# A Flamingo block with a mixture of experts on one core: the last batch's two head groups are worked side by side

## The reference, cut to what matters

```python
def _L1_xattn_ref(q, k, v):          # q: tokens x features, k = v = context
    qh = q.reshape(b * h, d // h, m)     # h = 8 heads of 32 tokens each
    qk = jnp.einsum('bdm,bdn->bmn', qh, kh) * scale
    sm = jax.nn.softmax(qk, axis=-1)     # 512 x 512 for each head
    ret = jnp.einsum('bmn,bcn->bcm', sm, vh)
    return ret.reshape(b, c, m)

def _L1_ffn_ref(x, w_gate, w_shared_up, w_shared_down, w_up, w_down):
    su = x_flat @ w_shared_up            # the shared expert
    y_s, g_s = jnp.split(su, 2, axis=-1)
    shared = jax.nn.silu(g_s) * y_s @ w_shared_down
    scores = jax.nn.sigmoid(x_flat @ w_gate)
    _, topk_idx = jax.lax.top_k(scores, TOPK)
    ...
    pos = jnp.take_along_axis(jnp.cumsum(oh, axis=0), flat_e[:, None], axis=1)[:, 0] - 1
    x_disp = jnp.zeros((E, CAP, C), x.dtype).at[flat_e, pos].set(x_flat[token_ids], mode='drop')
```

## Time and profile before

| what | value |
|---|---|
| three runs | 1053.34, 1055.82, 1057.88 us (median 1055.82) |
| the profiled execution | 1054.74 us, of which the trace's span is 1053.0 us |
| PE busy | 993.8 us (94%) |
| DVE, ACT, POOL busy | 603.7, 335.0, 465.5 us |
| last batch's own stretch | about 643 to 723 us of the span |

### The profile page before, as it was taken

How to read it: one execution, slowest core, us unless ns; L and a number is a source line. 1 busy time by engine, 2 the same in 40 slices (tenths; PEclk the granted TensorE clock), 3 DMA queues, 4 the chain that set the end, 5 groups by cost and what they waited for, 6 DMA issues and landing times.

```text
span 1053.0 us, 15353 instructions
## 1 busy us (share of the span) xinstructions
PE 993.8 (94%) x5629; PEld 606.8 (58%) x5630; DVE 603.7 (57%) x1249; ACT 335.0 (32%) x491; POOL 465.5 (44%) x457
## 2 busy tenths in 40 slices
PE   7999899999999999999999998895999999999887
PEld 6986445554554564564464462344777777776432
DVE  3334454675765765855846756743655556553566
ACT  3411023323224133233223332442434444443221
POOL 1000023724756657567577553462355555556000
PEclk9999899999999999999999999997999999999999
DMA  8893268598682581590530327556899999965998
GB/s 316 292 390 115 83 221 333 206 346 329 222 303 100 190 309 45 193 350 1 188 116 32 103 80 305 204 210 253 300 370 383 376 370 372 372 250 214 376 417 324
DMA packets 93622, 262.23 MB, mean 249 GB/s; under 512 B 10454, under 2 KB 10582, under 8 KB 92784
## 3 DMA queue, kind: packets, MB, share of 16 engines
q1 hardware_dynamic: 43760, 146.18, 38.0%
q10 hardware_dynamic: 31872, 63.97, 16.2%
q0 software_dynamic: 17920, 51.15, 12.4%
HBM read 129.91 MB, written 139.72 MB: 256 GB/s over the span
## 4 chain that ended last, share of the span: by engine, by line
PE 71%; DVE 7%; POOL 7%; DMA 7%; issue 4%; ACT 3%; SPq 0%; POOLq 0%; ACTq 0%; DVEq 0%
PE banks L1266 17%; PE banks L1861 11%; PE banks L1276 10%; PE banks L1850 6%; DMA e_eo<-y_d 6%; PE banks L1870 6%; POOL t_psum L766 5%; PE banks L1364 5%; PE banks L1426 5%; PE banks L1444 2%; DVE t_nmx L1057 2%; ACT t_probs L857 2%; PE banks L396 1%; PE banks L402 1%; PE banks L407 1%
## 5 line engine op out<-in xcount | busy, mean ns | idle before, releaser
L1684 POOL DMA_INDIRECT y_d<-e_eo,e_ids x128 | 124.5, 972 | 126.7 <-DVE e_eo L1781 94.0
L1057 DVE TENSOR_REDUCE t_nmx<-banks 128x4 f32<-128x2048 f32 x56 | 128.1, 2288 | 61.2 <-PE banks L1364 61.2
L766 POOL TENSOR_TENSOR t_psum<-t_psum,t_probs 128x512 f32<-128x512 f32 x104 | 128.5, 1267 | 63.4 <-ACT t_probs L857 62.6
L857 ACT ACTIVATE t_probs<-banks 128x2048 f32<-128x2048 f32 x56 | 105.2, 1878 | 141.0 <-PE banks L1429 117.1
L778 POOL DMA_INDIRECT xs_d<-r_norm,r_xaddr x96 | 96.4, 1004 | 46.5 <-issue 24.9
L736 POOL TENSOR_TENSOR f_rstd<-f_veps,mhalf 128x2 f32<-128x2 f32 x24 | 16.8, 699 | 149.0 <-DVE f_veps L955 149.0
L1426 PE MATMUL banks<-b_qry,b_key 32*128 32x512 f32 x512 | 73.0, 639 | 7.8 <-ACT t_probs L857 5.7
L1850 PEld LDWEIGHTS banks<-ident,e_xg 128*128 128x128 f32 x512 | 57.4, 144 | 32.6 <-issue 32.5
L1850 PE MATMUL banks<-ident,e_xg 128*128 128x128 f32 x512 | 64.4, 281 | 10.9 <-DMA e_xg<-xs_d 10.9
L766 POOL TENSOR_TENSOR t_psum<-t_probs,t_probs 128x512 f32<-128x512 f32 x52 | 66.5, 1315 | 12.1 <-DVE b_qry L1047 6.0
L1364 PE MATMUL banks<-b_key,b_qry 32*128 32x512 f32 x448 | 65.0, 650 | 7.0 <-DVE t_nmx L1057 5.3
(11 more groups left out here) (223 smaller groups left out, 1633.0 us busy)
## 6 DMA issues: line engine op xcount, KB each, us to landing
xs_d<-zero ACTq DMA_DIRECT2D x32, 1056.0 KB, 6.7
e_xg<-xs_d SPq DMA_DIRECT2D x32, 1056.0 KB, 16.6
...
```

Source lines behind the costliest of these rows:

```text
L766: ins = g_.tensor_tensor(psum0[:, q, :], first[:, q, :], probs[s % NP][:, q, :], ALU.add)
L857: A(probs[s % NP][:, :, :], quad[:, :, :], ACT.Exp, scale=SCALE1).then_inc(W["exp_ok"], 1)
L1057: V.tensor_reduce(nmx[g][:, m, :], quad[:, :, :], axis=AX.X, op=ALU.max, negate=True).then_inc(W["mx_ok"], 1)
L1684: g_.indirect_dma_start(out=y_d, out_offset=bass.IndirectOffsetOnAxis(ap=ids[:, HC * p + n:HC * p + n + 1], axis=0), in_=eo[u][:, n, :], i ...
```

## The change

The list `ENDING` is rewritten from `L.S1a` on. In batch 7 the first four exps and products (`L.Q0` to `L.Q3`, `L.V0` to `L.V3`) now stand between the score pieces of the second group, which for this are all halves (`L.S4a` to `L.S7b`), so that `quad` is free for `L.Q0` to `L.Q3`. `L.S3` becomes whole. There are 13 pieces where there were 11. The group's row sums go to GpSimd (`L.sum0a` to `c`) with one product `L.Z0`; group 1 keeps its sums on PE. `L.up1` is also cut in quarters, and both cut products stand between the score pieces; behind `L.V7` there is `L.up2` alone. Batch 6's turns, router and sends (`R.turnA` to `R.x3`) come later. On GpSimd `L.stats1` stands before the six sends of `L.rows0a` and `L.rows0b`, which so join up with those of `L.rows1`. ACT copies batch 6's last product (`L.K1/6`) after the row of maxima. SP loads three weight pairs and the accumulators after `T.cT` (`L.more`).

```diff
-L.V6/7 L.pos0/7 L.slots0/7 L.rows0a/7 L.V7/7 L.up1/7 L.A1/7 L.up2/7 L.add1/7 L.stats1/7 L.rows0b/7 L.norm1/7 L.turn1/7 L.gates1/7 L.top1/7 L.pos1/7 L.slots1/7 L.rows1/7
+L.slots0/7 L.V7/7 L.up2/7 L.A1/7 L.add1/7 L.stats1/7 L.rows0a/7 L.rows0b/7 L.norm1/7 L.turn1/7 L.gates1/7 L.top1/7 L.pos1/7 L.slots1/7 L.rows1/7
...
-    ("L.S0", 0, 0, False), ("L.S1a", 1, 0, True), ("L.S1b", 1, 1, True), ("L.S2", 2, 0, False), ("L.S3a", 3, 0, True), ("L.S4", 4, 0, False),
-    ("L.S3b", 3, 1, True), ("L.S5", 5, 0, False), ("L.S6a", 6, 0, True), ("L.S7", 7, 0, False), ("L.S6b", 6, 1, True)))}
-CHOSEN = {("L.V4", 6): 2, ("L.up0a", 7): 3, ("L.M0", 7): 2, ("R.turnA", 6): 3, ("R.turnB", 6): 2}
+    ("L.S0", 0, 0, False), ("L.S1a", 1, 0, True), ("L.S2", 2, 0, False), ("L.S1b", 1, 1, True), ("L.S3", 3, 0, False),
+    *((f"L.S{n}{'ab'[half]}", n, half, True) for n in range(KC, 2 * KC) for half in range(2))))}
+CHOSEN = {("L.V4", 6): 2, ("L.up0a", 7): 1, ("L.M0", 7): 0, ("L.up1a", 7): 2, ("R.turnA", 6): 2, ("R.turnB", 6): 2, ("R.gates", 6): 2}
...
+def nth_sum(b, g):
+
+    return 2 * b + g - (b == LB)
+
+
+def by_pool(b, g):
+
+    return g == 0 or b < LB - 1
...
+        def more_ahead(b):
+            pairs_ahead(3, 6)
+            for u in range(2):
+                sp.wait_ge(W[f"accst{u}"], 16 * 2)
+            early_acc(0, 4)
...
+               "L.sum0a": sum_up(0, 1), "L.sum0b": sum_up(0, 2), "L.sum0c": sum_up(0, 3),
...
+                if n >= KC:
+                    act.wait_ge(W["sum_ok"], 3 * nth_sum(b, 0) + (1, 1, 2, 3)[n - KC])
                 act.wait_ge(W["st_mm"], 8 * b + n + 1)
...
-                dve.wait_ge(W["mx_ok"], 8 * b + (KC * (g + 1) if b < LB else (7, 11)[g]))
+                dve.wait_ge(W["mx_ok"], 8 * b + (KC * (g + 1) if b < LB else (5, 13)[g]))
...
+                if name == "L.S4a":
+                    pe.wait_ge(W["mrow_ok"], 2 * b + 1)
+                    pe.wait_ge(W["raw_ok"], 1)
...
-                dst = open_bank(f"T.Z{g}", b)
-                pe.wait_ge(W["sum_ok"], 3 * (2 * b + g) + 3)
+                dst = open_bank(f"{'TL'[b == LB]}.Z{g}", b)
+                pe.wait_ge(W["sum_ok"], 3 * nth_sum(b, g) + 3)
...
+            stages[f"L.V{n}"] = last_weighted(n) if n >= KC else weighted(n)
```

More of the change, by code:

```diff
@@ L505, in occupants @@
             lent = True
-        elif name == "L.S6b":
+        elif name == "L.S7b":
             holder[0:2] = [(name, b)] * 2
@@ L687, in first_pairs, with pairs_ahead @@
                 sp.wait_ge(W[n], 2 * NB)
+            pairs_ahead(0, 3)
+        def pairs_ahead(first, end):
             wu, wd, both = pair_weights(v)
-            for p in range(len(wu)):
+            for p in range(first, end):
                 load_pair(sp, io, both, w_in, p)
@@ L714, in shared_rows @@
                 sp.dma_start(nrT[k][:, :, :], nrT_d[c, :, :].rearrange("p (k s) -> p k s", k=KC)).then_inc(W["nr_in"], 16)
-        steps({"F.keys": f_keys, "F.down1": loads_ahead, "T.cT": t_values, "F.next": f_next, "R.acc": r_acc, "R.keep": r_keep, "L.load": shared_rows})
+        steps({"F.keys": f_keys, "F.down1": loads_ahead, "L.more": more_ahead, "T.cT": t_values, "F.next": f_next, "R.acc": r_acc, "R.keep": r_keep, "L.load": shared_rows})
         sp.wait_ge(W["pv_mm"], 8 * NB)
@@ L757, in stage @@
                 if n == 1:
-                    since(pool, W["z_mm"], 2 * b + g)
+                    since(pool, W["z_mm"], nth_sum(b, g))
                     first = probs[(s - 1) % NP]
@@ L1501, in shared_up, with shared_up_part @@
             return stage
[L1503 to L1504 removed]
+        def shared_up_part(c, part):
+            j = part // 2
             def stage(b):
[L1507 to L1513 removed]
+                if part == 0:
+                    if c == 0:
+                        pe.wait_ge(W["nr_in"], 16 * (len(UPS) - 1))
+                        pe.wait_ge(W["mx_ok"], 8 * b + PIECES["L.S1b"][0] + 1)
+                    open_bank(f"L.up{c}a", b)
+                for k in range(2 * (part % 2), 2 * (part % 2) + 2):
+                    ins = mm(bank(f"L.up{c}a", b)[:, j * S:(j + 1) * S], wsu[:, k, j * P:(j + 1) * P], nrT[c][:, k, :], start=(k == 0), stop=(k == KC - 1))
+                if part == 3:
                     ins.then_inc(W["su_mm"], 1)
@@ L1542, in tensor @@
             stages[f"L.pos{t}"] = last_pos(t)
-        for c in range(1, len(UPS)):
-            stages[f"L.up{c}"] = shared_up(c)
-        for c in range(4):
-            stages[f"L.up0{'abcd'[c]}"] = first_shared_up(c)
+        for c in range(len(UPS)):
+            if c in PARTED:
+                for part in range(4):
+                    stages[f"L.up{c}{'abcd'[part]}"] = shared_up_part(c, part)
+            else:
+                stages[f"L.up{c}"] = shared_up(c)
+        stages["L.Z0"] = sums(0)
         for n in range(KC * NG):
-            stages[f"L.V{n}"] = last_weighted(n)
+            stages[f"L.V{n}"] = last_weighted(n) if n >= KC else weighted(n)
             stages[f"T.S{n}"] = scores(n)
```

48 lines of the change are left out of this document (17 added, 31 removed), and 4 rows, old and new, of the table RELEASES.

## The result

The kernel after takes 1058.84 us, the median of 16 runs (1057.23 to 1063.09); the kernel before, run beside it, takes 1055.74 (16 runs, 1053.34 to 1059.34). The ratio is 1.0039, 95% interval 1.0029 to 1.005. The medians differ by 3.1 us and the means by 4.1: within the 0.5% that I called no change, but a real loss. I had predicted 1056.6, which is 0.8 us above the median of before.

What follows compares the result with a forecast made beforehand. PE was taken to bound the kernel (busy 993.8 of 1053.0 us). Work of 55.8 plus 2.9 us idle put L.V7 0.8 us later, with the tail as long as before: median 1055.82 becomes 1056.6 us, range 1051.5 to 1061.0.

Steps and rivals of the forecast that it cites:

- What bounds the stretch: Ahead of L.V7's end PE is busy 51.98 of 57.83 us, so overlapping exps can win at most 5.85 us.
- The work: PE up to L.V7: 51.98 + 2.1 (pieces) - 2.5 (row sums) + 4.2 (L.up1) = 55.8 us.
- rival 1: The first four exps vanish behind the maxima: L.V7 earlier, 6 us faster, 1049.8; chance 0.05.
- The idle time: PE's waits up to L.V7: 0.1 + 0.7 + 0.2 + 1.7 + 0.2 = 2.9 us, instead of 5.85.
- the walk: Steps through the new list by prices, each unit starting at the later of PE's last one and its wait; gave the idle 2.9 us.
- rival 2: GpSimd's sums hold up PE at L.Z0, or DVE falls behind the halves; over 0.5% slower, chance 0.09.
- Sum for the order: L.S0 to L.V7's end: 55.8 us work + 2.9 idle = 58.7 instead of 57.83, put at 0.8 us later.
- The tail: Behind L.V7, twelve sends in a row on GpSimd start the last at +19.5 us (+19.4 before), eating the 0.9 us won.
- GpSimd's other work: Ahead of the tail: three sums from 668.0 to 682.9, 1.2 us to spare before L.Z0; batch 6's addresses at 688.2.

Runs made afterwards that it cites:

- e11: From e7: batch 6's norm put ahead of L.S5a's maximum on DVE, and GpSimd's first sum waits for it; 1069.17 us, ratio 1.0043 to before.
- e3: Kernel after with GpSimd's three row sums of the last batch cut to 8 of 512 columns; 1069.75 us, ratio 1.0045 to before.
- e8: Kernel after with the last batch's first-group row sums moved from GpSimd to PE, 16 products in L.Z0; 1061.62 us, ratio 1.0059 to before.
- e9: The same edit to the kernel after as e3, run in another lot; 1067.84 us, ratio 1.0035 to before.
- e4: Kernel after with batch 6's norm moved behind L.S5a's maximum on DVE, and GpSimd's first sum waiting for it; 1075.21 us, ratio 1.0094 to before.
- e1: Kernel after, unchanged, on a slower chip where all engines stop for some 5 us; 1071.4 us, ratio 1.0082 to before.
- e6: Kernel after, unchanged, run again on an undisturbed chip; 1059.2 us, ratio 1.0044 to before.
- e5: Kernel before, unchanged, run again on an undisturbed chip; 1055.01 us, ratio 1.0002.
- e2: Kernel after with batch 6's first transposes issued four times over on PE ahead of L.S7a; 1072.9 us, ratio 1.0074 to before.
- e10: From e8: DVE takes a tile's statistics three times more behind batch 6's norm, into an unread place; 1073.48 us, ratio 1.0077 to before.
- e7: Kernel after with L.up1 whole behind L.V7 again, as in before; 1058.41 us, ratio 1.0036 to before.

## Why the prediction was right, and where it was not

**What bounds the stretch** was right: there were 5.85 us to win on PE, PE's work sets the rest, and 3 us of the idle time could not be worth more than they are.

**The work.** I had 55.8 us; at full clock it is 32.89 + 21.89 = 54.8. Most prices held (a half 1.06, `L.V0` to `L.V3` 1.00, the last exps' steps); a quarter between score pieces took 1.06 where I had 1.14. What I had not priced: a half piece runs at the same time as two products of the next `L.Q` (660.57 and 660.58, 670.02 and 670.05 above). To judge by the starts these are the products of the two heads whose rows of the array the half leaves free; they start 0.5 us ahead of the half's own last two (661.10), which stand before them in the queue. A half and an `L.Q` take 2.14 us together (`L.V0` at 662.71, `L.S4b` at 660.57) where I had 1.06 + 1.29. A trifle in the direction of rival 1, which otherwise fell: `L.V7` ended later, not 6 us earlier.

**The idle time** is the term that was mis-sized. I had 2.9 us; at full clock it is 2.09 + 2.50 = 4.6. Ahead of `L.M1` 0.55 (0.7 forecast), ahead of `L.Q5` 1.7 to 1.8 (1.7), ahead of `L.S6b` 0.25 (0.1): all in place. Missing in the walk is `L.S7a`'s 1.84. I let DVE's norm for batch 6 take its 1.0 + 0.2 us of before, and asked about GpSimd's sums only whether DVE would lengthen *them*. It was the other way round: the two sums together took 10.38 us (10.05 in e11, where only their end met a step of DVE's), the norm 3.6 instead of 1.2. e3, e8 and e9 show it by taking the adds away, and e4 and e11 by moving the norm out of their way. In these last two the sums then ran beside the split `L.P1`, and it was the split that took 1.0 to 1.7 us more. I had named "a DVE that falls behind the halves" in rival 2 at under 0.09 and priced its slack at 0.2 us; it came, at 1.8 us.

The Trainium skill, "SBUF — State Buffer", section Who interferes with whom, lists DVE's `tensor_scalar` among the operations that can take the port shared with GpSimd, and says that who issues first blocks the other for the whole instruction, and that a reduction never contends. The rows agree: of the norm's two pieces, 0.54 us each in e9, one took 0.93 and the other 1.50 in e1, and the reductions stayed at 1.22. I had used the rule in one direction alone, for the sums' length.

**Sum for the order:** +1.5 us where I had +0.8. That the two are so close is partly luck: 1.7 us too little idle time against 1.0 us too much work. And the time as a whole lies in my range because the range was wide: the change is 3 to 4 us, four to five times the 0.8 of the forecast. `L.V7` ended at 706.8 in the profile, not at 701.5 to 702.5 as I had it, and the last send started at 726.5, not near 721.5.

**The tail** was right: twelve sends in a row, last send +19.7 (+19.5 forecast), the freed 0.9 us eaten. GpSimd was even idle 2.25 us ahead of the second power, where I had it 0.4 in front of it: most likely because the low clock had delayed `L.V7` and not the sends.

**GpSimd's other work**: sums 665.4 to 680.9 (forecast 668.0 to 682.9), `L.Z0` never waited; addresses at 691.3 (688.2), 3 us late by the clock.

**What I did not have at all** is the clock. In the two profiles with a mean of 0.978 it takes 5.4 us up to `L.V7`, and in the experts 0.7 us in the first and 1.4 in e6 (325.5 us from the first turn to the end, against e5's 324.1). Does it balance? In the group at the higher clock the median is 1058.4, 2.6 above before: 1.5 from the order, 0.3 from the tail, 0.7 from the start of the experts. But this leaves out the second low stretch, at `L.Q5` (1.4 us, 5.4 - 4.0). If the group has it as well, as most profiles do, the sum is 3.9, and 1.3 us too high; that is open. The group at the lower clock is 4 us above the other, and in it there are 13.6 us at 1.2 GHz between `L.S7a` and `L.V7`, of which the first 10.2 cost 4.0. That the higher group lacks just that stretch is inferred from its mean clock (0.005 of 1058 us is 10.6 us at half clock); no profile on an undisturbed chip is of that group.

**Is the low clock the order's doing?** The evidence leans to yes, and isn't complete. For: in after and e6 the stretch of 10.2 us starts 3.3 us behind the start of the idle time ahead of `L.S7a`; where that idle time is absent or filled (e2, e3, e8, e9, e11) none starts between there and `L.Q4`; put back by other means (e10) it is there again. In e5 the fall starts 3.4 us behind the start of such an idle time, one of 1.13 us. The steadiest case is another one, the wait ahead of `L.Q5`, 1.7 to 1.8 us in every profile of the new order, where before's exps let PE wait 0.3 us at most. In eleven of the twelve profiles of the new order and its variants a fall starts there, between 0.3 us ahead of the start of `L.Q5` and 1.8 us behind it, of 3.4 us in nine and 6.8 us in two; only e1 has none, and before has none in either profile. I had this wait in the walk, at 1.7 us, but not its clock. Against: e1 has the idle time and no stretch, e7 has it and only 3.4 us, 8 us later; and before, whose order has four idle times of 0.8 to 1.4 us, got a stretch in e5 and not in its first profile. That an idle time on PE makes a fall of the clock likelier fits all of this, from one profile for each run; what decides in one execution stays open.
